# A two-layer attention and expert kernel on one core: the padding of two operands cleared one buffer at a time, and the planned order made from other costs

## The reference

```python
xn = _layernorm(x)
s = _L0_attn_ref(xn, ...)          # 16 heads of 8, rope, causal softmax, output projection
g = _silu(_L0_ffn_ref(xn, ...))    # soft experts: 8 experts x 64 slots
x = x + s * g
xn = _layernorm(x)
s = _L1_attn_ref(xn, ...)          # as in layer 0, other weights
g = _silu(_L1_ffn_ref(xn, ...))    # 16 experts, top 2 per row, top 512 rows per expert, layer norm
x = x + s * g
```

## Time and profile before

| | |
|---|---|
| median of 3 runs | 673.24 us (672.61 to 675.51) |
| the profiled execution | 673.67 us |
| its span, first to last instruction | 671.9 us |
| mean granted PE clock | 0.983 |
| instructions | 14420 |

### The profile page before, as it was taken

How to read it: one execution, slowest core, us unless ns; L and a number is a source line. 1 busy time by engine, 2 the same in 40 slices (tenths; PEclk the granted TensorE clock), 3 DMA queues, 4 the chain that set the end, 5 groups by cost and what they waited for, 6 DMA issues and landing times.

```text
span 671.9 us, 14420 instructions
## 1 busy us (share of the span) xinstructions
PE 608.0 (90%) x4988; PEld 287.5 (43%) x5052; DVE 534.6 (80%) x933; ACT 457.6 (68%) x907; POOL 217.2 (32%) x355
## 2 busy tenths in 40 slices
PE   0487899999999999999999999989999999999993
PEld 0344566643535334443524434333333333337652
DVE  7866657769887888979688888899989889854875
ACT  0365547678577877778676857787777787785782
POOL 5558641011120226473201256642032230221032
PEclk9879999999999999999999999999999999999997
DMA  6045925313130403063404630353141420300001
GB/s 185 0 162 153 199 80 180 105 34 71 34 96 9 104 22 83 2 165 119 108 6 97 174 79 13 100 161 97 39 102 38 69 66 9 71 3 1 1 17 47
DMA packets 36012, 52.11 MB, mean 78 GB/s; under 512 B 5992, under 2 KB 27400, under 8 KB 33672
## 3 DMA queue, kind: packets, MB, share of 16 engines
q1 hardware_dynamic: 34648, 50.74, 28.7%
q10 hardware_dynamic: 1296, 0.46, 0.3%
HBM read 37.29 MB, written 13.63 MB: 76 GB/s over the span
## 4 chain that ended last, share of the span: by engine, by line
PE 72%; DVE 9%; ACT 5%; POOL 4%; issue 4%; DMA 3%; SPq 2%; another core or an unknown queue 0%; POOLq 0%; ACTq 0%; DVEq 0%
PE ps L1336 66%; ACT probs L1045 2%; DVE maxes L1320 2%; PE ps L1555 2%; DMA F<-in_spread 1%; PE ps L1428 1%; SPq L820 1%; POOL xn L571 1%; ACT F L983 1%; POOL F L921 1%; DMA F<-in_w 1%; PE ps L1390 1%; DVE bnst L1081 1%; PE ps L1444 1%; DVE root L1146 1%
## 5 line engine op out<-in xcount | busy, mean ns | idle before, releaser
L1320 DVE TENSOR_REDUCE maxes<-ps 128x2 f32<-128x1024 f32 (+3 forms) x292 | 340.2, 1206 | 49.4 <-PE ps L1336 45.9
L1045 ACT ACTIVATE probs<-ps 128x512 f32<-128x512 f32 x576 | 307.6, 602 | 80.9 <-PE ps L1336 69.3
L1336 PE MATMUL ps<-qop,kop 128*128 128x512 bf16 (+3 forms) x704 | 162.0, 324 | 7.0 <-ACT probs L1045 3.0
L882 POOL TENSOR_SCALAR_AFFINE_SELECT probs<-probs 128x512 f32<-128x512 f32 (+1 forms) x160 | 84.6, 550 | 232.7 <-ACT probs L1045 232.6
L1336 PE MATMUL ps<-probs,vals 128*9 128x512 f32 (+3 forms) x1536 | 152.6, 488 | 3.3 <-issue 0.9
L1336 PE MATMUL ps<-kmx,qmx 32*128 32x128 bf16 (+2 forms) x1280 | 104.7, 261 | 4.6 <-DVE maxes L1320 2.8
L1336 PEld LDWEIGHTS ps<-qop,kop 128*128 128x128 bf16 x768 | 59.7, 99 | 83.5 <-ACT probs L1045 45.0
L1336 PEld LDWEIGHTS ps<-kmx,qmx 32*128 32x128 bf16 x1280 | 38.6, 92 | 116.3 <-issue 64.9
L1336 PE MATMUL ps<-F 128*128 128x128 f32 (+2 forms) x640 | 75.5, 279 | 5.1 <-ACT F L983 4.3
L1336 PEld LDWEIGHTS ps<-F 128*128 128x128 f32 (+2 forms) x640 | 66.9, 176 | 22.3 <-issue 12.5
L1336 PEld LDWEIGHTS ps<-probs,vals 128*9 128x9 f32 x1536 | 27.1, 89 | 59.8 <-issue 40.6
(11 more groups left out here) (157 smaller groups left out, 607.7 us busy)
## 6 DMA issues: line engine op xcount, KB each, us to landing
qop<-q_thirds SPq DMA_DIRECT2D x42, 192.0 KB
kop<-k_thirds SPq DMA_DIRECT2D x42, 192.0 KB
F<-in_w SPq DMA_DIRECT2D x16, 256.0 KB, 4.3
qmx<-q_thirds SPq DMA_DIRECT2D x14, 256.0 KB
kmx<-k_thirds SPq DMA_DIRECT2D x14, 256.0 KB
q_thirds<-third SPq DMA_DIRECT2D x8, 384.0 KB, 5.0
k_thirds<-third SPq DMA_DIRECT2D x8, 384.0 KB, 2.9
q_thirds<-third SPq DMA_DIRECT2D x8, 256.0 KB, 3.0
```

The source lines that it names most:

```text
L882: last = pool.affine_select(where, where, [[0, number], [1, P]], ALU.is_ge, 0.0, base=0, channel_multiplier=-1)
L1045: act.activation(probs[:, u % RING, :], bank(at), ACT.Exp, scale=SCALE).then_inc(s_cells_read, 1)
L1320: dve.tensor_reduce(dst, src, AX.X, ALU.max).then_inc(s_units_read[pair // 2], 1)
L1336: return pe.matmul(out_, lhsT, rhs, start=first, stop=last)
```

## The change

The three memsets are split and moved. `pad(r)` clears one buffer of `kop` and of `qop`, now over all 128 partitions. `pad(0)` runs first, then the memset of `vals`; `pad(1)` becomes a step of `ORDER`, `("pad",)`, which needs `emb` and which the `ldexp` of group 1 needs. `ldexp` of group 0 waits for 2 counts of `s_ones` and that of group 1 for 4. `v` stays in the same row of steps as `xT` and `qk`. The planner's prices, `HOP`, `TILING`, `COLUMN`, `STAY` and all bonuses in `MORE` are other numbers. Arithmetic and work are otherwise the same; the order of the steps on all engines is what the planner makes of the new numbers.

```diff
-HOP, TILING, COLUMN, COLUMN4, LAND, FIRST = 0.2, 0.1, 0.000425, 0.0017, 3.0, 3.0
+HOP, TILING, COLUMN, COLUMN4, LAND, FIRST = 0.12, 0.095, 0.000418, 0.00168, 3.0, 3.0
...
-STAY = {"whole": 110.0, "rows": -5.0, "columns": -4.0, "halves": 10.0, None: 0.0}
+STAY = {"whole": 80.0, "rows": 61.0, "columns": 61.0, "halves": 10.0, None: 0.0}
...
-    "embT": -109, "embstat": -96, "eo": 118, "es": -56, "exp": (-79, -106), "halve": (-21, 62), "heads": (-42, -120),
+    "emb": 143, "embT": -60, "embstat": -120, "eo": 142, "es": 150, "exp": (1, -66), "halve": (160, -45),
...
-    "ldmax": (-10, 100), "ldw": 65,
-    "ldwA": 103, "ldwB": 117, "left": (4, -22, 69), "lg": -115, "limit": 2, "ln": -23, "lnroot": -86, "lnstat": -109,
-    "logit": 145, "low": (82, 121, -9), "lt": -14, "mask": (-75, 33), "max": (-2, 72), "middle": (-107, -57, 100),
-    "mix": -66, "norm": (46, -26, 134), "offs": 144, "out": (-42, -8), "proj": (150, -120), "pv": (-113, -120),
+    "ldmax": (-84, 141), "ldw": 45, "ldwA": -113, "ldwB": -4, "left": (106, 156, 41), "lg": -116, "limit": -113, "ln": 107,
+    "lnroot": 113, "lnstat": 151, "logit": -45, "low": (-57, -48, 46), "lt": 37, "mask": (158, -81), "max": (4, 47),
+    "middle": (-92, 47, -13), "mix": -2, "norm": (-120, 134, -115), "offs": -120, "out": (69, -73), "pad": 94,
+    "proj": (20, -12), "pv": (-103, -79), "pvout": (3, 83), "qk": (-71, 43, 78), "rT": 124, "rden": (114, 84), "res": -120,
...
-    "emb": (0, "", (("POOL", 4.9),)),
-    "diag": (0, "", (("POOL", 2.0),)),
+    "emb": (0, "", (("POOL", 6.0),)), "pad": (0, "", (("POOL", 3.6),)),
+    "diag": (0, "", (("POOL", 2.85),)),
...
-    "lnroot": (0, "", (("DVE", 2.4),))
+    "lnroot": (0, "", (("DVE", 2.5),))
...
-        return COLUMN * BANK, "A", (("ACT", 0.54),)
+        return COLUMN * BANK, "A", (("ACT", 0.51),)
...
-        return 0, "", (("DVE", 2.4) if what[1:] == (0, 0) else ("POOL", 2.4),)
+        return 0, "", (("DVE", 2.5) if what[1:] == (0, 0) else ("POOL", 3.5),)
...
-    if kind == "embT":
+    if kind in ("embT", "pad"):
         return [("emb",)]
...
-        return [("ldmax", n, c)] + ([("exp", n - 2, NU - 1)] if n >= 2 else [])
+        return [("ldmax", n, c)] + ([("exp", n - 2, NU - 1)] if n >= 2 else [("pad",)] * n)
...
-                        sp.wait_ge(s_ones, 2)
+                        sp.wait_ge(s_ones, 2 * n + 2)
...
+            def pad(r):
+                done = 2 * r
+                pool.memset(kop[:, r].rearrange("p h t -> p (h t)").bitcast(F32), ONES).then_inc(s_ones, 1)
+                pool.wait_ge(s_ones, done + 1)
+                pool.memset(qop[:, r].rearrange("p h t -> p (h t)").bitcast(F32), 0.0).then_inc(s_ones, 1)
+                pool.wait_ge(s_ones, done + 2)
+
+            pad(0)
             pool.memset(vals[:, :, :, :, :], 1.0).then_inc(s_pad, 1)
             pool.wait_ge(s_pad, 1)
-
-            pool.memset(kop[64:P].rearrange("p r h t -> p (r h t)").bitcast(F32), ONES).then_inc(s_ones, 1)
-            pool.wait_ge(s_ones, 1)
-            pool.memset(qop[64:P].rearrange("p r h t -> p (r h t)").bitcast(F32), 0.0).then_inc(s_ones, 1)
-            pool.wait_ge(s_ones, 2)
...
+                elif kind == "pad":
+                    pad(1)
```

More of the change, by code:

```diff
@@ L150 @@
 MORE = {
-    "add": (147, -34), "attT": (43, 160), "colsum": 104, "count": 150, "ct": 125, "diag": -99, "disp": -118, "emb": -72,
-    "embT": -109, "embstat": -96, "eo": 118, "es": -56, "exp": (-79, -106), "halve": (-21, 62), "heads": (-42, -120),
-    "hid": -64, "hid1": -116, "high": (44, 124, 85), "ldexp": (73, 94), "ldf1": 87, "ldmax": (-10, 100), "ldw": 65,
-    "ldwA": 103, "ldwB": 117, "left": (4, -22, 69), "lg": -115, "limit": 2, "ln": -23, "lnroot": -86, "lnstat": -109,
-    "logit": 145, "low": (82, 121, -9), "lt": -14, "mask": (-75, 33), "max": (-2, 72), "middle": (-107, -57, 100),
-    "mix": -66, "norm": (46, -26, 134), "offs": 144, "out": (-42, -8), "proj": (150, -120), "pv": (-113, -120),
[L157 to L160, removed]
+    "add": (144, 135), "attT": (-22, 82), "colsum": -39, "comb": 86, "count": -114, "ct": 50, "diag": 121, "disp": -103,
+    "emb": 143, "embT": -60, "embstat": -120, "eo": 142, "es": 150, "exp": (1, -66), "halve": (160, -45),
+    "heads": (-99, 67), "hid": -53, "hid1": -78, "high": (55, 108, -42), "ldexp": (-48, 116), "ldf1": -52,
+    "ldmax": (-84, 141), "ldw": 45, "ldwA": -113, "ldwB": -4, "left": (106, 156, 41), "lg": -116, "limit": -113, "ln": 107,
+    "lnroot": 113, "lnstat": 151, "logit": -45, "low": (-57, -48, 46), "lt": 37, "mask": (158, -81), "max": (4, 47),
+    "middle": (-92, 47, -13), "mix": -2, "norm": (-120, 134, -115), "offs": -120, "out": (69, -73), "pad": 94,
+    "proj": (20, -12), "pv": (-103, -79), "pvout": (3, 83), "qk": (-71, 43, 78), "rT": 124, "rden": (114, 84), "res": -120,
+    "root": (-52, 60), "routes": 160, "rs": 63, "shift": (-21, -42), "silu": (-11, 88), "slot": -111, "soft": 118,
+    "stat": (83, -77, -11), "store": (74, 45, 96), "sum": (-11, 122, -86), "top": (-40, 47), "total": 116,
+    "v": (-106, -77, -12), "wg": 23, "xT": (70, -30, 133), "xr": 150, "xrT": 85, "z": 82,
 }
@@ L176 @@
     "stat": (0, "", (("DVE", 2.8),)), "embstat": (0, "", (("DVE", 2.4),)),
[L177 to L178 removed]
+    "emb": (0, "", (("POOL", 6.0),)), "pad": (0, "", (("POOL", 3.6),)),
+    "colsum": (0, "", (("DVE", 0.2),)), "diag": (0, "", (("POOL", 2.85),)), "rs": (0, "", (("DVE", 0.2),)), "rden": (0, "", (("DVE", 0.6),)), "heads": (0, "", (("POOL", 1.1),)),
     "routes": (0, "", (("DVE", 2.3),)), "count": (0, "", (("DVE", 1.7),)), "limit": (0, "", (("DVE", 2.2),)),
[L180 removed]
+    "lnstat": (0, "", (("DVE", 2.8),)), "lnroot": (0, "", (("DVE", 2.5),)), "ln": (0, "", (("DVE", 1.0),)), "top": (0, "", (("DVE", 0.3),)), "halve": (0, "", (("POOL", 0.5),)),
     "high": (0, "", (("ACT", 0.63),)), "middle": (0, "", (("ACT", 0.63),)), "silu": (0, "", (("ACT", 3.7),)),
@@ L195, in cost @@
         pieces = pattern(arg[0])[arg[1] // 2]
-        masks = 2 * COLUMN * BANK + TILING + 0.1 if pieces in DIAGONALS else 0.0
+        masks = 2 * COLUMN * BANK + TILING if pieces in DIAGONALS else 0.0
         return COLUMN * sum(w for _, _, w in pieces) + masks, "D", (("DVE", 0.1 + 0.0022 * sum(w for _, _, w in pieces)),)
@@ L385, in streams @@
     made += [[("xr", c), ("xrT", c)] for c in range(4)]
-    made.append([("embstat",), ("emb",), ("embT",)])
+    made += [[("embstat",), ("emb",), ("embT",)], [("pad",)]]
     made.append([("lt", u) for u in range(B * NB0)])
```

## The result

| | before | after |
|---|---|---|
| median of 12 runs each | 673.24 us (671.61 to 675.61) | 680.33 us (676.39 to 683.77) |
| ratio | | 1.0094 (95%: 1.0070 to 1.0119) |
| the profiled execution, its span | 673.67, 671.9 us | 678.31, 676.6 us |
| mean granted PE clock | 0.983 | 0.979 |

The change made the kernel slower by 0.94%; the forecast was 666.4 us, range 658 to 676. The profiled execution of after lies 2.0 us under the median of its runs.

The account below looks back on a forecast made before the run. PE's own stream was taken to bound 100 to 600 us, with other idle time at the ends. Terms -2.8 + 1.0 - 1.5 - 3.5 = -6.8 gave 666.9 us profiled, 666.4 against the median; range 658 to 676.

Parts of the forecast that it names:

- Term 1: Memsets at the start: a shorter first pair ends a DVE TENSOR_SCALAR's wait, PE's first matmul moves with it; -2.8 us.
- Term 2: Second pair of memsets, after `emb` on POOL: free in POOL's gap, 3.6 us at most; taken as +1.0 us.
- Term 3: PE's order in the opening: told higher POOL costs, the planner may put another transpose ahead of `embT`; -1.5 us.
- Term 4: Changes of tiling on PE, 0.10 us each: new STAY saves 35, mostly in layer 1; -3.5 us, bounds +3 and -9.
- The other new numbers: Within term 4: HOP, `exp` and COLUMN prices move what the planner thinks ready; 0, bounds -3 and +4 us.
- Term 5: The end: last `heads` on POOL waits behind an `add`; nothing in the diff prefers it first; 0, bounds -2.5 and +2.5.
- ACT is starved by runs of `pv`: Rival, layer 1: products joined four at a time keep PE from `exp`, ACT idles; 677 to 681 us, chance 0.13.
- The order gives nothing: Rival: only the start gains, PE's idle rest need not shrink; -2.8 + 1.0 = -1.8, 671.4 us, chance 0.25.

## Why the prediction was wrong

**Term 1, the memsets (-2.8): right**, in mechanism and size: 6.52 for the end of `vals` (6.5), 0.17 for the second TENSOR_SCALAR, and PE's first matmul at 13.86 (13.9).

**Term 2, the second pair (+1.0): mis-sized.** The prediction put the pair's price nearer to the gap "since POOL waits for ACT between most of those steps", though it had itself said that the bonuses put the pair ahead. It cost all that term 1 wins, 2.8 us, in before's list; in after's the same step is not clear of noise (0.7 to 2.2). In before's list the sum of terms 1 and 2 is 0, and not -1.8.

**Term 3, PE's order (-1.5): right in kind, too small.** `embT` waits 0.6 where it waited 9.1, and the first logits' product starts 3.6 us earlier although the pair stands ahead. With terms 1 and 2 I had -3.3 for the opening; PE is 3.2 us of work ahead at 100. What reaches the end is less: before's kernel with the new opening is 0.19% under before, 1.3 us, and not clear of no gain.

**Term 4, changes of tiling (-3.5): right in size, wrong in place.** By the weight loads they fell from 728 to 684, by 44 (35 predicted): 28 of them between 100 and 430 us and only 16 between 430 and 600, where I looked. In layer 1, 15 steps of `pv` join the one before in place of 2 (26 predicted), and `max` joins more often in both layers, where I expected nothing new. Between 125 and 600 the changes are 37 fewer, worth 3.7 us at 0.10 each, and the account shows 2.4 won; the 1.3 between them is not traced. No run has the fewer changes without the list they come with, so the saving by itself is argued, not shown.

**"The other new numbers": 0, bounds -3 and +4. This is the first step that failed.** I priced the new list by its changes and its estimates, and took the waits of PE from before's profile as if they came along. The list brought a wait of its own: weights issued close behind group 2's operands, which come 3.7 us late, then a clock at half. That is 4.1 us lost between 100 and 125; another 1.4 went between 600 and 640, which no run traces. In the trace of before the wait did not show, since the operands were issued 6 us ahead of the weights and the list held two more units of `max` there. The kernel with the operands behind the weights and these units put back is 5.9 us faster than after: mending this one place wins back most of the 7.1 us by which after is slower.

**Term 5, the end: 0, bounds ±2.5. The second step that failed**: 4.7 us in the profiles, and 6.8 for the new end in before's list, outside the bounds. I had looked at what an order could win there (POOL's last `heads`) and had set the same for what it could lose. But the end is a chain over DVE, POOL, ACT and PE with no cover, and its steps' bonuses (`lnstat`, `lnroot`, `ln`, `rden`, `heads`) changed by up to 260. Which of the steps costs how much is only in part shown: the late reciprocal is worth some 1.9 us.

Without these two steps the profiles' account would be -3.2 - 2.4 = -5.6 against the -6.8 forecast.

**The rivals.** "ACT is starved by runs of `pv`" named 677 to 681, where the time came out, but not why: PE's waits for ACT's `probs` are 1.5 us in all, where before had 4.0, and the new list has no run of four `pv` steps and one of three. "The order gives nothing" was right in that the second pair takes the start's gain, and missed that an order can cost. No case of mine held the mechanism that decided. A rival "the new list brings a wait on a transfer" would have been drawn from the 1.1 us by which expert 4's weights are in ahead of their use in before (119.3 to 120.42), from the 0.24 us that PE waits for expert 5's, and from SP's queue. The planner does not see it: `LAND`, its price for a transfer, is 3.0 us in both kernels, and the one that decided took 8.95.

**What stays open.** The middle and the end each cost 7 to 8 us alone and no more together; why they don't add is only argued (cut lists don't fit, and a shorter end needs work that is ready at 640). Whether the order of the loads would do for the middle without the filler was not tried. With three of its places mended the new list stands at 672.0, the old one with the same memsets at 669.9: its remaining 2.1 us, inside overlapping intervals, were not traced to a step. Nor were the 2.0 us between after's profiled run and its median: its 12 runs had mean granted clocks of 0.970 to 0.981, with spans of 682.0 down to 674.6, and only the profiled run shows where the clock fell.

## What to carry to other kernels

A list made by another set of planner's numbers is another kernel: count not only what it saves, but look in the old trace for each wait that is hidden by a few us of lead (here the 1.1 us by which weights had landed ahead of their use, and a lead of 6 us of the operands' load over theirs), and give the ends, which nothing covers, a bound for losses as wide as the chain there is long. A memset that is moved off the start must be put into a gap by its place in the queue; beside a chain that everything waits for, it can cost all that the early start wins (here 2.8 of its 3.6 us). And test a saved quantity alone: here 28 fewer changes of tiling came with 56 us more, in waits and at the lower clock.

## What the runs showed of the hardware

**Two-input DVE operations stand still beside a POOL add, but not beside a POOL memset.** In after's last 20 us the TENSOR_TENSOR of L563 on 4 elements takes 1.20 us beside an operation of POOL's `add` that takes 1.26, and 0.16 at 660.80 with POOL idle. In before, while POOL writes `qop` (6.43 to 9.94), such an operation takes 0.16 us, and the TENSOR_SCALAR behind it 3.12:

```profile
6.64 0.16 DVE L1145 TENSOR_TENSOR root<-root,mv 128x4 f32<-128x4 f32 x1
```

The Trainium skill ("SBUF — State Buffer", "SBUF: two separate sides") says that a DVE operation with two inputs in SBUF is held only by a GpSimd operation that reads SBUF. The trace agrees: 1.20 us beside the `add`, which reads two tiles, and 0.16 beside the memset, which reads none.

**A load issued close behind another landed later.** The four blocks of expert weights had a median of 7.0 us from issue to landing with group 2's operands issued 2 to 4 us ahead of them, and 3.5 us with the operands issued after them.

**A short wait was followed by a slower clock.** After 3.66 us of idle PE at 115 the granted clock was at 1.2 GHz for 3.4 us; with two units of filler in that place it stayed at 2.4 GHz from 46.5 to 657.4 us. In the split-memsets kernel the clock fell at 444.8 us for 6.8 us where the longest idle stretch of PE since 100 us was 1.2: the trace does not show why every fall comes.
